# A transformer block on one core: attention outputs without transpositions, a feed-forward part in row and column tiles, and another preparation of the first batch

## The reference

```python
qkv = _layernorm(x) @ qkv_w.T + qkv_b          # 16 heads of 16
q, k = rope(q), rope(k)
scores = q @ k.T * 0.25, masked above the diagonal
attn = softmax(scores) @ v                      # 8 batches x 16 heads of 1024 x 1024
x = x + _layernorm(attn @ proj_w.T + proj_b)
P = _layernorm(x) @ U1                          # 256 -> 64
H = gelu(P @ V1 + b1)                           # 64 -> 1024
x = x + _layernorm((H @ U2) @ V2 + b2)          # 1024 -> 64 -> 256
```

## Time and profile before

| what | us |
|---|---|
| median of 3 runs (1441.19 to 1446.45) | 1443.12 |
| the profiled execution | 1444.75 |
| its span | 1442.9 |
| TensorE busy | 1320.8 (92%) |
| VectorE busy | 1070.2 (74%) |
| ScalarE busy | 872.5 (60%) |
| GpSimd busy | 603.3 (42%) |
| mean granted TensorE clock | 0.957 |

### The profile page before, as it was taken

The page is one execution under the profiler, slowest core; times in us unless marked ns, Lnnn a source line. Parts: engine busy times, 40 slices in busy tenths (PEclk is TensorE's granted clock), DMA queues, the critical chain, the costliest instruction groups (busy, mean ns, idle before and its releaser), DMA issues.

```text
span 1442.9 us, 30280 instructions
## 1 busy us (share of the span) xinstructions
PE 1320.8 (92%) x12592; PEld 609.8 (42%) x12592; DVE 1070.2 (74%) x1800; ACT 872.5 (60%) x1200; POOL 603.3 (42%) x521
## 2 busy tenths in 40 slices
PE   4678999999999999999999999999999989999994
PEld 1323444444444444444444444444444433555441
DVE  4765777867777786877687778777788986647778
ACT  3214766657665766676677667766666767665451
POOL 5556482226534462446245634553411323222334
PEclk9768999989999999999999999999999999999997
DMA  4382453344435353544353435353454530212112
GB/s 157 100 148 91 75 122 87 60 91 75 104 60 119 68 111 61 119 76 104 60 119 75 104 60 120 75 105 60 93 72 61 108 91 2 74 48 84 59 45 101
DMA packets 79805, 124.21 MB, mean 86 GB/s; under 512 B 14006, under 2 KB 49972, under 8 KB 79668
## 3 DMA queue, kind: packets, MB, share of 16 engines
q1 hardware_dynamic: 79668, 122.28, 39.8%
HBM read 70.85 MB, written 50.33 MB: 84 GB/s over the span
## 4 chain that ended last, share of the span: by engine, by line
PE 65%; POOL 12%; ACT 9%; DVE 6%; issue 4%; DMA 3%; SPq 2%; DVEq 0%; ACTq 0%; POOLq 0%
PE PV L993 15%; PE RING L953 10%; PE RING L979 10%; ACT PB L1334 6%; PE MI L918 6%; PE RING L1051 4%; PE MI L1017 4%; POOL TA L749 2%; PE MI L928 2%; POOL TB L751 2%; PE RING L1044 2%; PE RING L1045 2%; PE RING L1035 2%; POOL PB L1404 2%; PE RING L960 2%
## 5 line engine op out<-in xcount | busy, mean ns | idle before, releaser
L1334 ACT ACTIVATE PB<-RING 128x1024 f32<-128x1024 f32 (+2 forms) x640 | 581.9, 939 | 291.7 <-PE RING L979 287.8
L1127 DVE TENSOR_REDUCE M<-RING 128x2 f32<-128x1024 f32 (+3 forms) x448 | 499.2, 1143 | 146.6 <-PE RING L960 73.1
L993 PE MATMUL PV<-PB,V 128*17 128x512 f32 (+3 forms) x3072 | 328.8, 507 | 6.8 <-POOL PB L1404 5.9
L953 PE MATMUL RING<-QK 48*128 48x512 f32 (+3 forms) x1536 | 300.2, 410 | 36.5 <-DVE M L1127 15.0
L1404 POOL TENSOR_SCALAR_AFFINE_SELECT PB<-PB 128x512 f32<-128x512 f32 x256 | 163.3, 641 | 390.4 <-ACT PB L1334 390.2
L979 PE MATMUL RING<-QK 50*128 50x512 f32 (+3 forms) x1536 | 280.7, 406 | 11.6 <-ACT PB L1334 7.0
L1127 DVE TENSOR_REDUCE MB<-RING 128x2 f32<-128x768 f32 (+2 forms) x192 | 197.4, 1042 | 70.9 <-PE RING L960 69.8
L953 PEld LDWEIGHTS RING<-QK 48*128 48x128 f32 x1536 | 149.1, 192 | 188.7 <-issue 65.4
L979 PEld LDWEIGHTS RING<-QK 50*128 50x128 f32 x1536 | 134.2, 189 | 175.7 <-ACT PB L1334 73.4
L960 PE MATMUL RING<-MASKK,MASKQ 64*128 64x64 bf16 x2048 | 122.7, 200 | 0.0
L918 PE MATMUL MI<-XT,WQ 128*32 128x512 f32 x896 | 114.4, 630 | 2.3 <-ACT EO L1307 1.6
(11 more groups left out here) (111 smaller groups left out, 1386.5 us busy)
## 6 DMA issues: line engine op xcount, KB each, us to landing
QK<-split_parts SPq DMA_DIRECT2D x372, 128.0 KB, 5.8
split_parts<-PARTS SPq DMA_DIRECT2D x64, 256.0 KB, 3.5
split_parts<-EO SPq DMA_DIRECT2D x64, 256.0 KB, 4.3
block_mid<-Y SPq DMA_DIRECT2D x16, 512.0 KB, 4.1
F_X<-block_mid SPq DMA_DIRECT2D x16, 512.0 KB, 5.7
X<-x SPq DMA_DIRECT2D x7, 1024.0 KB, 9.7
out<-F_Y SPq DMA_DIRECT2D x14, 512.0 KB, 2.9
QK<-NSROW SPq DMA_DIRECT2D x128, 8.0 KB, 1.9
```

Source lines behind the costliest of these rows:

```text
L953: ins = e.matmul(m[:, h, i, :], QK[g % 3][r, 0, k, 128 * t:128 * t + 128], QK[g % 3][r, 1, k, k0:k0 + n], start=True, stop=not open_end(g, s))
L993: ins = e.matmul(PV[32 * h:32 * h + 17, off:512], V[b % 2][:, j, 4 * (g % 4) + h, :], PB[(SLOTS * g + s) % 4][:, h, 0:n], start=(j == 0), ...
L1127: e.tensor_reduce(acc, ring(("max", g, s, u), pairs, n), AX.X, ALU.max).then_inc(v_max, 1)
L1334: e.activation(buf[:, :, pairs[0]:pairs[-1] + 1, :], ring(("score", g, s, u), pairs, n), ACT.Exp).then_inc(a_exp, 1)
```

## The change

1. **Behind a product.** The values get 16 columns of ones for every two heads (`VL`, `VU`: 25 blocks of 16 columns, of which every third holds ones), so that a product of 32 columns gives 16 rows of values and 16 equal rows of sums. `OT` is no longer transposed: five transfers ("att_load") copy it from SBUF to SBUF, the values to `ATT[c]` and the sums to `SUM[c]`. VectorE takes the reciprocal of a whole `SUM[c]` ("att_inverse", 128 x 512, once for every two groups and c), and GpSimd multiplies ("att_scale"). Steps "ot", "ot_out", "att" and "att_out" are gone. The upper halves of the values have one buffer for all batches.
2. **Masks.** Where a "max" step holds two head pairs, one mask product covers both.
3. **Feed-forward part.** "up" takes three products of 64 rows for each a, in two row tiles; "f_u1" makes both halves in one step, in two column tiles; "f_y" takes 64 rows for each a. "f_norm" moves to ScalarE, and rounds end in two halves.
4. **First batch.** Half c = 1 gets buffers of its own (`PB[0]`, `PB[1]`), all rotations and rests go to VectorE, all roundings to ScalarE, and the masks' copies stand behind the first half's work.
5. **Plan.** Due times come from a table `DUE` and from `pace`, transfers have a modelled rate, and `LAG`, `LEAD`, `LOAD` are 3.95, 15.08 and 20.76.

```diff
-SLOTS, LAG, LEAD, LOAD = 12, 3, 15, 21
+SLOTS, LAG, LEAD, LOAD = 12, 3.95, 15.08, 20.76
+DUE = {"ln_stats": (-10.78, 5.44), "ln_dev": (-9.94, -0.47), "ln_rows": (-7.23, 5.21), "xt": (-5.06, 16.12),
...
 def rope_by(b, c, p):
-    return "DVE" if b == 0 and c == p else "POOL"
+    return "DVE" if b == 0 else "POOL"
 def round_by(b, c, p):
-    return "ACT" if b == 0 and c != p else "DVE"
+    return "ACT" if b == 0 else "DVE"
...
+        def fine(b, c):
+            return PB[0] if (b, c) == (0, 1) else EO
...
+                elif what == "att_load":
+                    g, c = at
+                    k, r0 = g % 4 // 2, 64 * (g % 2)
+                    w.wait_ge(a_ot, 2 * g + c + 1)
+                    if g >= 2:
+                        w.wait_ge(g_att, NTH["att_scale", (g // 2 - 1) // 2, c, (g // 2 - 1) % 2])
+                    if g >= 4:
+                        w.wait_ge(p_mi["proj"], NTH["proj", g // 4 - 1, c, 2])
+                    w.wait_ge(v_mask, 1)
+                    for r, p0 in ((0, 16), (32, 80)):
+                        e.dma_start(ATT[c][r0 + r:r0 + r + 32, k, :], OT[p0:p0 + 32, :]).then_inc(s_att[c], 16)
+                    for r, p0, n in ((0, 0, 16), (16, 48, 32), (48, 112, 16)):
+                        e.dma_start(SUM[c][r0 + r:r0 + r + n, :], OT[p0:p0 + n, :]).then_inc(s_att[c], 16)
...
-                            for z in range(2):
-                                for h in range(2):
-                                    r = slice(64 * h, 64 * h + 64)
-                                    ins = e.matmul(m[:, h, i, n - 128 + 64 * z:n - 64 + 64 * z], MASKQ[r, z, :],
-                                                   MASKK[r, z, :], start=False, stop=(z == 1))
+                        for z in range(2):
+                            for h in range(2):
+                                r = slice(64 * h, 64 * h + 64)
+                                ins = e.matmul(m[:, h, :, n - 128 + 64 * z:n - 64 + 64 * z], MASKQ[r, z, :],
+                                               MASKK[r, z, :].unsqueeze(1).to_broadcast([64, len(pairs), 64]),
+                                               start=False, stop=(z == 1))
...
-                        ins = e.matmul(PV[32 * h:32 * h + 17, off:512], V[b % 2][:, j, 4 * (g % 4) + h, :],
+                        n0 = 48 * (2 * (g % 4) + h // 2) + 32 * (h % 2)
+                        ins = e.matmul(PV[32 * h:32 * h + 32, off:512], v[:, n0:n0 + 32],
...
-                    for k in range(2):
-                        ins = e.matmul(PP[:, :], U1[:, k, :], FXT[:, k, :], start=(k == 0), stop=(k == 1))
+                    for k in range(2):
+                        for a in range(2):
+                            ins = e.matmul(TP[64 * a:64 * a + 64, :], U1[:, k, :], FXT[a][:, k, :], start=(k == 0), stop=(k == 1))
...
-                    e.matmul(m[:, :], V1A[:, 128 * f:128 * f + 128], p[:, :], start=True, stop=False)
-                    e.matmul(m[:, :], V1B[:, 128 * f:128 * f + 128], p[:, :], start=False, stop=True).then_inc(f_v1, 1)
+                    terms = ((V1A, FP[i % 2][0]), (V1A, FP[i % 2][1]), (V1B, FP[i % 2][0]))
+                    for n, (v, p) in enumerate(terms):
+                        for a in range(2):
+                            r = slice(64 * a, 64 * a + 64)
+                            ins = e.matmul(m[a][:, :], v[r, cols], p[r, :], start=(n == 0), stop=(n == 2))
...
-                    e.matmul(YP[j % 2][:, :], FQ[i % 2][:, 128 * j:128 * j + 128], V2[:, :],
-                             start=True, stop=True).then_inc(f_v2, 1)
+                    for j in range(2):
+                        q = 128 * (2 * u + j)
+                        for a in range(2):
+                            r = slice(64 * a, 64 * a + 64)
+                            ins = e.matmul(YP[a][:, 256 * j:256 * j + 256], FQ[i % 2][r, q:q + 128], V2[r, :], start=True, stop=True)
...
+                    w.wait_ge(s_att[1 - c], 80 * (g + c))
                     e.activation(OT[:, :], PV[:, :], ACT.Copy).then_inc(a_ot, 1)
...
+                elif what == "att_inverse":
+                    w.wait_ge(s_att[c], 80 * (4 * b + 2 * k + 2))
+                    e.reciprocal(SUM[c][:, :], SUM[c][:, :]).then_inc(v_inv, 1)
...
+                elif what == "att_scale":
+                    w.wait_ge(v_inv, NTH["att_inverse", b, c, k])
+                    e.tensor_tensor(ATT[c][:, k, :], ATT[c][:, k, :], SUM[c][:, :], ALU.mult).then_inc(g_att, 1)
```

More of the change, by code:

```diff
@@ L70, in prep_times, with pace @@
+def pace(columns):
+    work = [[2 * len(u) * n + EACH for u in units(n)] for n in columns]
+    total, at, out = sum(map(sum, work)), 0, []
+    for w in work:
+        out.append([])
+        for x in w:
+            out[-1].append(EVEN * (at / total * SLOTS) + (1 - EVEN) * (len(out) - 1 + (len(out[-1])) / 2))
+            at += x
+    return out
 def prep_times(b):
     if b == 0:
-        steps = [("ln_stats", 0, 0, j) for j in range(4)] + [("ln_dev", 0, 0), ("ln_pow", 0, 0), ("ln_shift", 0, 0)]
@@ L120, in due_times @@
         if b >= 2:
[L121 removed]
+            at.append((PER * (b - 1) + DUE["load_x"][0], ("load_x", b)))
+    scores = pace([width(s)[3] for s in range(SLOTS)])
     for g in range(NG):
+        maxes = pace([reach(g, s)[3] for s in range(SLOTS)])
         if g:
@@ L305, in forward_needs @@
     if what in ("f_load", "f_zero"):
-        return [("values_out", last, 6), ("send", last, 1, 0), ("send", last, 1, 1), ("residual", last - 1, 1, 2)]
+        return [("values_out", last, 6), ("send", last, 1, 0), ("send", last, 1, 1), *[("residual", last - 1, c, 2) for c in range(2)],
+                ("score", NG - 3, SLOTS - 1, 0)]
     if what == "f_fill":
@@ L428, in cost @@
         masked = what == "max" and open_end(*at[:2])
-        return pairs * (10 * n // 24 + 15 + 170 * masked)
+        return pairs * (10 * n // 24 + 15 + 30 * masked) + 150 * masked
+    if what in ("rope", "rest") and at[0] == 0:
+        return 1400 if what == "rope" else 1250
+    if what == "round" and at[0] == 0:
+        return 1060
     if what == "product":
@@ L435, in tiling @@
 def tiling(step):
-    return {"score": "rows", "max": "rows", "product": "columns", "down": "columns"}.get(
+    return {"score": "rows", "max": "rows", "up": "rows", "f_y": "rows", "product": "columns", "down": "halves", "f_u1": "halves"}.get(
         step[0], "columns" if step[0] in ("qk", "values", "fold", "proj") else "whole")
@@ L535, in order_of_work @@
         free[engine] = start + took
-        done[step] = start + took + LATE[engine]
+        if engine == "SP":
+            size, rate, late = MOVES[step[0]]
+            if step[0] == "load_group" and step[2] is not None:
+                size //= 2
+            moved = max(moved, start + 500) + size / rate
+            done[step] = max(start + took + late, moved + 1800)
+        else:
+            done[step] = start + took + LATE[engine]
         if step[0] in EMPTIES:
@@ L568, in block_kernel @@
     for what, *at in ORDER["SP"]:
-        if what == "send":
+        if what == "send" and tuple(at[:2]) != (0, 1):
             sent[at[2]] += 1
@@ L1390, in gpsimd @@
                 what, *at = step
-                if what == "ln_pow":
+                if what == "ones":
+                    w.wait_ge(g_rs, sum(s[0] == "ln_pow" for s in ORDER["POOL"][:ORDER["POOL"].index(step)]))
+                    ones(*at)
+                elif what == "ln_pow":
                     b, c = at
```

524 lines of the change are left out of this document (253 added, 271 removed), and 3 rows, old and new, of the table DUE.

## The result

| | before | changed |
|---|---|---|
| median of 20 runs each, us | 1444.64 (1438.35 to 1460.38) | 1455.5 (1445.29 to 1475.42) |
| ratio of the times, 95% interval | | 1.0058 (1.0037 to 1.008) |
| first to last exponential start | 123.1 to 1224.5: 1101.4 | 97.4 to 1288.6: 1191.2 |
| first to last gelu start | 1229.7 to 1411.0: 181.3 | 1292.6 to 1448.7: 156.1 |

The forecast was 1323. The change is slower than before by 0.6%, just outside what can be told from no change. The profiled execution of the changed kernel is its longest, 1475.42 us, and one of four slower ones that the ratio leaves out, so some 20 us of what its rows show is not in the median.

What follows compares the result with a forecast made beforehand. TensorE was taken to bound the groups and feed-forward part, waits the beginning. Groups 58, beginning 30 and feed-forward part 32 make 120 us off 1444.75, 1325; with the median 1.6 lower, 1323, range 1268 to 1380.

Steps and rivals of the forecast that it cites:

- Beginning, -30: First batch: earlier norm, rotations on VectorE and closer half loads bring the first score 30 us earlier (bounds 18 and 38).
- Feed-forward part, -32: Feed-forward rounds: row and column tiles save TensorE work, 4.0 us a round, 32 us for eight (bounds 18 and 43).
- (a): Rival: other engines take over, VectorE's reciprocal and ScalarE's rounds; groups give 35, feed-forward part 18: 1360 us; chance 0.21.
- How much of that comes back: I take 85%, 68 us.: Groups: of 80 us of work leaving TensorE, 85% returns as time, 68 us; ends 45% (VectorE at its limit) and 100%.
- The masks: Groups: one wide mask product for two pairs saves 0.12 us in each of 128 steps, 15 us of TensorE work.
- I take 0.7.: Groups, VectorE: the 128 x 512 reciprocal takes 0.7 us, chosen between 0.687 from below and 3.1 from above.
- I book 0.3 us for each of the 32 groups, 10 us.: Groups: OT copies behind a group load are sometimes late, costing 0.3 us a group, 10 us in all.
- (c): Rival: slower, the OT copy late in each group and holding up ScalarE and TensorE: 1467 us; chance 0.03.
- The plan: New order of nearly every instruction: no term of its own; named as why the groups' returning share was trusted least.
- (b): Rival: all comes back and TensorE's gaps partly close; groups 95, beginning 34, feed-forward part 42: 1272 us; chance 0.15.
- (d): Rival: no change; TensorE's records overlap so the transpositions cost little, and the new order costs the rest; chance 0.01.

Runs made afterwards that it cites:

- e6: Kernel before with the new first batch, new feed-forward part and wide mask products, otherwise the groups of before in their order: 1370.48 us, ratio 0.9479.
- e17: e6 in frozen order, transpositions behind the products and their followers removed, PV copied straight to ATT at wrong rows, no transfers or division: 1384.01 us, 0.9599.
- e1: Changed kernel with the reciprocal replaced by a multiplication of the same tile, instruction order kept: 1419.59 us, 0.9833.
- e16: e6 in frozen order, transpositions behind the products replaced by the transfers, without the division and its VectorE and GpSimd steps: 1475.73 us, 1.0252.
- e2: Changed kernel with only the planner's cost of the reciprocal set to 3350 instead of 650, so only the order moves: 1522.17 us, 1.0539.
- e8: Changed kernel with the old due times, LAG, LEAD and LOAD of the attention's steps: 1527.38 us, 1.0517.
- e18: Changed kernel without its reciprocals and scalings, in its own order: 1419.29 us, 0.9863.
- e3: Changed kernel with part 1 undone (transpositions and small VectorE steps back), new due times kept: 1462.26 us, 1.0133.
- e7: Changed kernel with a second OT buffer, the planner's rule about OT gone too: 1503.37 us, 1.0414.
- e13: Changed kernel with two buffers for the upper half's values, due at 34.15 in place of 63.28: 1470.77 us, 1.0185.
- e15: e6 with part 1 put in by frozen order, ScalarE issuing the transfers and the division's steps placed a little later: 1714.29 us, 1.1883.

## Why the prediction was wrong, by its steps

- **Beginning, -30.** The first score came 25.9 us earlier, and in e6 the first exponential 29.2 earlier (93.9). The time is right, in part by luck: the first maxima of c = 1 start at 69.28 in place of 85.99, 16.7 us earlier and not 27 ("that is 27 us"), and the stretch from there to the first score, which was to keep its 37 us, took 27.4.
- **Feed-forward part, -32.** The gelus' stretch is 25.2 us shorter in the changed kernel, and 1192.2 to 1343.6, 29.9 us shorter, in e6. Right in kind; 2 to 7 us too much. ScalarE is busy for 15.2 of 20 us there (the mean of 1340 to 1360 and 1360 to 1380), where TensorE has 19.4, so it doesn't hold TensorE up as (a) feared. The tail, which was to keep its steps, became 6.9 us shorter (25.0 behind the last gelu's start in place of 31.9), so that the part as a whole gave its 32.
- **"How much of that comes back: I take 85%, 68 us."** This is the step that failed. The work of the transpositions was right, 65 us, and e17 took them out with nothing in their place, in the same order, and with VectorE's and ScalarE's steps behind them: the time rose by 17 us, and nothing came back. The masks say the same: booked with 15 us of work, they were worth 4 to 6 (e6). The view was read wrongly: TensorE's 137.05 of 143 us, with a fifth to spare on the others, was taken as TensorE being the bound. The reading that fits e17's rows: TensorE was busy because a filler stood between its maxima and scores, and those depend on VectorE and ScalarE through the three pairs of banks of `RING`. With the filler gone it waits for them (26 us more), and its clock is lower more often (96 us for 51), so that the work that is left takes longer. That the waits are what lowers the clock is not shown by itself. The range's lower end of 45% was no bound; the row that excludes a loss does not exist.
- **"I take 0.7."** The reciprocal takes 3.347 us. The upper bound of the same paragraph, from the 16-element row's 0.092 us, was 3.1 and nearly right; the choice between the ends was not. The 5.75 ns an element were real: (3347 - 155) / 512 is 6.2. The Trainium skill's repeat count of 8 (VectorE: DVE Perf Modes, First, the fixed hardware budget) gave 4.4 as an estimate; the measurement, 3.347 us, lies between, and nearer to the row's. By e1 it costs 32 us here.
- **"I book 0.3 us for each of the 32 groups, 10 us."** ScalarE's wait for these transfers is 17.2 us in the changed kernel, 0.5 a group, so the booking was of the right size and rival (c)'s threshold of 4.1 us a group was never met as a wait. But a wait need not be its price: in e16 49.1 us of it went with 94 us of time. That VectorE would wait for the same transfers, with maxima behind it, stood only in the rivals.
- **The plan.** The prediction trusted its effect least, rightly, and gave it no term. It has one as large as any other: with the same instructions the order alone moved the time by 69 us (e2), and by 66 with the due times (e8).
- **Rivals.** (a) named what took over, VectorE with a 3.1 us reciprocal between maxima, and its 1360 was far too near, because it kept three fifths of the gain in the groups. (b) has no support: in the groups nothing came back. (c)'s side, slower, was right, and of its mechanism the queue of transfers behind a group load is seen, at a smaller wait. (d), at 0.01, comes nearest: the transpositions' time did not come back, and much of the rest is the order's. Its reason, that the records overlap, is not the one that e17's rows show. That the time came out so near to that of before is chance: the ends' gain of some 50 us and the groups' loss nearly cancel.

What stays open: why exactly the changed kernel's groups, at 1.0058, lose 0.058 against e6 though its order suits part 1. The division is 0.020 of it (e18). For the rest, single undoings (e3, e7, e13) each made it slower or left it, and each of them moved the order, so I can't divide it between transfers, due times and the single upper buffer. A list for part 1 that is optimised around two `OT` buffers and short reciprocals wasn't tried.

## What to carry to other kernels

An engine at 96% with fillers between steps that others must empty is not proof of a bound: take the filler out in a frozen order (leaving the result unfinished) before building its replacement, and see what the waits and the granted clock do. Where a planner writes the lists, freeze its order for an experiment, since here one number of the planner moved the time by 69 us through the order alone. When a gain at the ends comes together with a loss in the middle, time the parts apart: here the parts that worked were worth 5.2%, and the whole lost 0.6%.

## What was not expected of the hardware

- An fp32 reciprocal of 128 x 512 on VectorE takes 3347 ns, 6.2 ns a column, where a 512-column addition takes 687 and the multiplication of the same tile in e1 684.
- One transfer of `OT` costs its queue 0.53 to 0.59 us to issue in e16's rows, also where it moves only 32 KB, and on ScalarE the compute instructions behind it wait for that (e15: 3.16 us for five).
- TensorE's granted clock fell in the middle of work, 30 times in the changed kernel's groups, and not only behind a long idle. In this timeline (start, duration) a pair of 512-column maxima or scores takes 0.50 us until 645.70 and 0.80 at 646.42; the granted clock is 1.00 from 643 to 646 us and 0.56 from 646 to 650. From 640 on TensorE stood idle for 0.27 us at most at a time. What it did differently before the fall is that from 641.77 to 645.70 such pairs started 0.43 to 0.70 us apart, with at most a mask product of 0.23 between two, where earlier, from 630 to 633, it had 44 matmuls in 3 us, and from 643 to 646 only 16:

```profile
644.87 0.23 PE L1026 MATMUL RING<-MASKK,MASKQ 64*128 64x64 bf16 x4
645.22 0.50 PE L1046 MATMUL RING<-QK 50*128 50x512 f32 x2
645.70 0.50 PE L1019 MATMUL RING<-QK 48*128 48x512 f32 x2
646.04 0.23 PE L1026 MATMUL RING<-MASKK,MASKQ 64*128 64x64 bf16 x4
646.42 0.80 PE L1046 MATMUL RING<-QK 50*128 50x512 f32 x2
```
